# The shared expert's activation is split without its product with ones, and the last step's splits change places

## What is computed

```python
def _gate(x, gate_w, gate_bias):
    ...                      # 8 of 64 experts a token, their weights
    return (tidx, tw * SCALE)
w_dense = jnp.zeros((T, E), tw.dtype).at[jnp.arange(T)[:, None], tidx].add(tw)
def body(acc, ws):
    wg, wu, wdn, cw = ws
    hmid = jax.nn.silu(x @ wg) * (x @ wu)
    return (acc + cw[:, None] * (hmid @ wdn), None)
y, _ = jax.lax.scan(body, jnp.zeros_like(x), (We_gate, We_up, We_down, w_dense.T))
shared = jax.nn.silu(hidden_states @ Ws_gate) * (hidden_states @ Ws_up) @ Ws_down
return y + shared
```

## Time and profile before

| | us |
|---|---|
| median of three runs | 858.88 |
| lowest and highest | 857.32, 859.14 |
| the profiled execution | 856.9 |
| its span, first to last instruction | 855.1 |
| PE busy within it | 831.7 |
| of the page's chain that ended last, PE | 86% |

### The profile page before, as it was taken

How to read it: one execution, slowest core, us unless ns; L and a number is a source line. 1 busy time by engine, 2 the same in 40 slices (tenths; PEclk the granted TensorE clock), 3 DMA queues, 4 the chain that set the end, 5 groups by cost and what they waited for, 6 DMA issues and landing times.

```text
span 855.1 us, 20312 instructions
## 1 busy us (share of the span) xinstructions
PE 831.7 (97%) x6781; PEld 652.9 (76%) x6781; DVE 684.0 (80%) x1641; ACT 568.5 (66%) x967; POOL 641.2 (75%) x606
## 2 busy tenths in 40 slices
PE   7999999999999999999999999999999999999997
PEld 5577767777766678888888888878888888888885
DVE  6899989999897779769679787867987967876665
ACT  4488888888878765575576566557557557655554
POOL 2778888888853478877777886877787778778785
PEclk8699999999999999999999999999999999999999
DMA  5667787877652266547456555654654745656562
GB/s 146 173 150 175 176 178 168 196 163 176 139 129 51 68 137 173 127 116 171 126 140 146 133 136 139 155 122 111 158 143 111 183 118 141 142 119 147 137 141 55
DMA packets 108035, 120.03 MB, mean 140 GB/s; under 512 B 28560, under 2 KB 70352, under 8 KB 106496
## 3 DMA queue, kind: packets, MB, share of 16 engines
q1 hardware_dynamic: 104816, 117.64, 57.8%
q10 hardware_dynamic: 3120, 1.18, 0.7%
HBM read 103.55 MB, written 14.71 MB: 138 GB/s over the span
## 4 chain that ended last, share of the span: by engine, by line
PE 86%; DMA 4%; DVE 4%; issue 2%; SPq 2%; ACT 1%; POOL 0%; DVEq 0%; ACTq 0%; POOLq 0%
PE bank L2019 20%; PE bank L2020 20%; PE bank L2021 20%; PE bank L1348 7%; PE bank L1335 5%; PE bank L1306 3%; PE bank L1288 2%; PE bank L1356 2%; PE bank L1272 1%; DMA stack_k<-k_scratch 1%; PE bank L1369 1%; PE bank L1282 1%; DMA k_scratch<-parts_k 1%; SPq L376 1%; DMA cwb<-wts_scratch 1%
## 5 line engine op out<-in xcount | busy, mean ns | idle before, releaser
L1696 POOL TENSOR_TENSOR hid<-act,cwb 128x512 f32<-128x512 f32 x264 | 425.2, 1620 | 124.3 <-DVE act L1923 69.6
L1749 ACT ACTIVATE silu<-bank 128x512 f32<-128x512 f32 x256 | 152.9, 597 | 191.9 <-PE bank L2021 187.7
L1923 DVE TENSOR_TENSOR act<-silu,bank 128x512 f32<-128x512 f32 (+1 forms) x264 | 180.4, 684 | 117.0 <-ACT silu L1749 77.4
L2019 PE MATMUL bank<-xhi,weights_hi 128*128 128x512 f32 x520 | 206.6, 397 | 0.5 <-ACT silu L1749 0.5
L1931 DVE TENSOR_TENSOR hlo<-hid,hhi 128x512 fp32r<-128x512 f32 x256 | 200.8, 785 | 7.1 <-ACT hhi L1755 6.9
L2021 PE MATMUL bank<-xlo,weights_hi 128*128 128x512 f32 x520 | 204.1, 393 | 0.0
L2020 PE MATMUL bank<-xhi,weights_lo 128*128 128x512 f32 x520 | 204.0, 392 | 0.0
L1755 ACT ACTIVATE hhi<-hid 128x512 fp32r<-128x512 f32 (+1 forms) x264 | 164.8, 625 | 14.0 <-POOL hid L1696 12.0
L1005 DVE TENSOR_REDUCE mx<-bank 128x4 f32<-128x512 f32 x240 | 156.0, 683 | 16.7 <-PE bank L1306 15.0
L796 ACT ACTIVATE prob<-bank 128x1024 f32<-128x1024 f32 x128 | 131.2, 1025 | 45.4 <-PE bank L1335 43.4
L2019 PEld LDWEIGHTS bank<-xhi,weights_hi 128*128 128x128 f32 x520 | 97.6, 188 | 22.1 <-ACT silu L1749 1.1
(11 more groups left out here) (242 smaller groups left out, 1037.4 us busy)
## 6 DMA issues: line engine op xcount, KB each, us to landing
cwb<-wts_scratch SPq DMA_DIRECT2D x174, 384.0 KB, 5.4
stack_k<-k_scratch SPq DMA_DIRECT2D x30, 256.0 KB, 4.4
k_scratch<-parts_k SPq DMA_DIRECT2D x15, 384.0 KB, 3.6
stack_q<-q_scratch SPq DMA_DIRECT2D x30, 128.0 KB, 2.9
stack_k<-k_scratch SPq DMA_DIRECT2D x30, 128.0 KB, 5.2
q_scratch<-parts_q SPq DMA_DIRECT2D x15, 192.0 KB, 3.4
xin<-in_x_dram SPq DMA_DIRECT2D x16, 128.0 KB, 2.9
cin<-in_ctx_dram SPq DMA_DIRECT2D x16, 128.0 KB, 3.1
```

The lines of the kernel that those rows point to most:

```text
L1696: pool.tensor_tensor(h_buf[k][:], a_buf[k][:], cwb[slot][:, q % GP, :], ALU.mult).then_inc(h_ok, 1)
L1749: act.activation(s_buf[k % RS][:], g_bank[k % 2][:], ACT.Silu).then_inc(s_ok, 1)
L1923: nc.vector.tensor_tensor(a_buf[k % RS][at], s_buf[k % RS][at], u_bank[k % 3][at], ALU.mult).then_inc(a_ok, 1)
L2019: nc.tensor.matmul(bank, w[0], mh, start=first, stop=False)
```

## The change

Three things, in words:

- The shared expert's activation is no longer multiplied by ones on POOL. ACT and DVE split `act` itself (`a_buf`) instead of `hid` (`h_buf`). POOL makes 32 products a chunk instead of 33, `h_ok` counts 32 a chunk, and all counts that are compared with it are changed. ACT's splits now name the product count as a value of their own (`done`). DVE gets a wait in step q = 2, that the split of the shared expert has read `act` before its buffer is written anew.
- The rows of ones are gone: `wT`, `f_wT` and `wts_scratch` have 64 rows, the write of ones on POOL and its waits are gone, and the last group of `cwb` in a chunk has two pairs instead of three.
- In the very last step of the last chunk, ACT does hhi of the third last pair ahead of the silu instead of after it, and DVE does its hlo ahead of the last act instead of after it.

```diff
@@ the write of ones, in the attention, on POOL @@
-                if n == NC - 2:
-                    pool.wait_ge(st_mm, UNITS * b)
-                    pool.wait_ge(xb_ok, n + 1)
-                    pool.memset(f_wT[E:NEX, :], 1.0).then_inc(fc_ok, 1)
-                    pool.wait_ge(fc_ok, 3)
@@ SP @@
         def load_cwb(c, gr, slot):
-            wait(sp, h_ok, NP * c + GP * (gr - 1))
+            wait(sp, h_ok, (NP - 1) * c + (GP * (gr - 1) if gr else -2))
+            q0, q1 = GP * gr, min(GP * (gr + 1), NP - 1)
             for half in range(2):
-                sp.dma_start(cwb[slot][half * F:(half + 1) * F, :, :],
-                             wts_v[c][half][GP * gr:GP * (gr + 1)].unsqueeze(0).to_broadcast([F, GP, T])
+                sp.dma_start(cwb[slot][half * F:(half + 1) * F, 0:q1 - q0, :],
+                             wts_v[c][half][q0:q1].unsqueeze(0).to_broadcast([F, q1 - q0, T])
                              ).then_inc(cw_in[slot], 16)
@@ POOL @@
-                for q in range(NP):
+                for q in range(NP - 1):
                     hidden(NP * c + q, q, j, g)
@@ ACT @@
-        def hid_hi(n, k):
-            at = slice(F if k % NP == NP - 1 else 0, P)
-            wait(act, h_ok, n + 1)
+        def hid_hi(n, k, done):
             wait(act, dn_mm, n + 1 - RH)
-            act.activation(hhi[k % RH][at], h_buf[k % RS][at], ACT.Copy).then_inc(hh_ok, 1)
+            if k % NP == NP - 1:
+                wait(act, a_ok, n + 1)
+                act.activation(hhi[k % RH][F:P], a_buf[k % RS][F:P], ACT.Copy).then_inc(hh_ok, 1)
+                return
+            wait(act, h_ok, done)
+            act.activation(hhi[k % RH][:], h_buf[k % RS][:], ACT.Copy).then_inc(hh_ok, 1)
...
-                    silu(n, k)
+                    end = not more and q == NP - 1
+                    if not end:
+                        silu(n, k)
                     if not (first and q < 2):
-                        hid_hi(n - 2, k - 2)
+                        hid_hi(n - 2, k - 2, (NP - 1) * c + max(q - 1, 0))
+                    if end:
+                        silu(n, k)
@@ DVE @@
-            wait(dve, h_ok, n + 1 - RS)
+            wait(dve, h_ok, hidden)
+            if k % NP == RS - 1:
+                wait(dve, hl_ok, n + 1 - RS)
...
-                nc.vector.tensor_tensor(hhi[k % RH][0:F], h_buf[k % RS][F:P], hhi[k % RH][F:P].bitcast(F32),
+                nc.vector.tensor_tensor(hhi[k % RH][0:F], a_buf[k % RS][F:P], hhi[k % RH][F:P].bitcast(F32),
...
-                    act_up(n, k, (NP - 1) * c + q)
+                    end = not more and q == NP - 1
+                    if not end:
+                        act_up(n, k, (NP - 1) * c + q, (NP - 1) * c + q + 1 - RS + (q < RS - 1))
...
                         hid_lo(n - 2, k - 2)
+                    if end:
+                        act_up(n, k, (NP - 1) * c + q, (NP - 1) * c + q + 1 - RS + (q < RS - 1))
```

More of the change, by code:

```diff
@@ L136, in build @@
         gwT = keep("gwT", [P, E], F32)
-        wts_d = nc.dram_tensor("wts_scratch", (NB // 4, NEX, 4 * P), F32, kind="Internal").ap()
+        wts_d = nc.dram_tensor("wts_scratch", (NB // 4, E, 4 * P), F32, kind="Internal").ap()
         cw_base = keep.at
@@ L269, in attention @@
     f_wsel, f_wnorm = f_masked, f_rep
-    f_wT = m_late("f_wT", [NEX, T], F32)
+    f_wT = m_late("f_wT", [E, T], F32)
     warm = m("warm", [P, 1], F32)
@@ L845, in first_wT @@
             act.wait_ge(fwt_mm, 1)
-            act.wait_ge(fc_ok, 3)
-            act.activation(f_wT[0:E, :], misc[0][0:E, :], ACT.Copy).then_inc(fwt_ev, 1)
+            act.activation(f_wT[:], misc[0][0:E, :], ACT.Copy).then_inc(fwt_ev, 1)
         evac_t(0, 0)
@@ L1740, in evac_w @@
             wait(act, wt_st, 16 * (c - 1))
-            act.activation(wT[0:E, :], misc[0:E, :], ACT.Copy).then_inc(wt_ev, 1)
+            act.activation(wT[:], misc[0:E, :], ACT.Copy).then_inc(wt_ev, 1)
         def silu(n, k):
@@ L1793, in on_act @@
         for q in range(2):
-            hid_hi(NP * NCH - 2 + q, 2 * NP - 2 + q)
+            hid_hi(NP * NCH - 2 + q, 2 * NP - 2 + q, (NP - 1) * NCH)
         wait(act, dn_mm, NP * NCH)
@@ L1915, in route, with act_up @@
                 tt(wnorm[:], wsel[:], wsum_p.unsqueeze(2).to_broadcast([P, K, E]), ALU.mult).then_inc(w_ok, 1)
-        def act_up(n, k, ups):
+        def act_up(n, k, ups, hidden):
             at = slice(F if k % NP == NP - 1 else 0, P)
```

## The result

| | before | after |
|---|---|---|
| median, 22 runs each | 857.17 | 860.75 |
| lowest and highest | 855.6, 859.54 | 857.7, 864.46 |
| the profiled execution | 856.9 | 862.24 |
| its span | 855.1 | 860.3 |

After takes 1.0041 times as long as before, with a 95% interval of 1.0031 to 1.0050: it is slower by 3.6 us. Its runs also spread wider, over 6.8 us for 3.9. The forecast was 857.9, in a range up to 860.0, with 0.08 for a slower kernel. The last step did become shorter, as forecast. But at the loop's turn, where the engines jump back to the start of its body, PE loses more than the change gains.

What follows compares the result with a forecast made beforehand. PE, busy 97% of the span, was taken as the bound. Gains of 0.90 us (last step) and 0.05 (rows of ones), all else 0, sum to 0.95, from a median of 858.88 to 857.9 us; range 856.0 to 860.0.

Steps and rivals of the forecast that it cites:

- The last step: End of the last chunk: without the eighth product and with the exchange, PE's last down starts 0.90 us earlier (0.6 to 1.3).
- Seven products at the chunks' ends: Chunk ends before another chunk: removing POOL's 1.8 us shared-expert products is hidden by PE's own work, worth 0.
- The slower rival: Loop's turn: ACT's body, grown by 64 instructions, makes a second code-fetch stand in each of two turns; 860.3 us, chance 8%.
- The rival of a shorter turn: Loop's turn: with less for POOL to do, PE's loss of some 1.2 us goes; gain 2.2, 856.7 us, chance 8%.
- The exchange alone: Last step: reordering silu, act and splits is itself worth -0.1 us; the product's removal brings all of the gain.
- The rows of ones: First chunk: 64 rows for 66 shorten the weights' store, 0.05 us reaching PE; dropping POOL's write of ones is worth 0.
- the added waits: ACT's extra register instruction per loop step and DVE's wait in step q = 2 fall in slack: cost 0.
- The signs named ahead: Trace signs at the last step, chunk ends, loop's turn and on POOL; a new ACT stand without releaser would refute the prediction.
- The long split: Last step, DVE: hlo of the third last pair takes about 1.7 us, not 0.69.
- the late act: Last step, DVE: the last act starts about 0.9 us later than silu allows.
- POOL's relief: Whole kernel: POOL's busy time falls by some 14 us.
- the stall at the turn: Loop's turn: PE's stall stays near 0.5 us.

## Why the prediction was wrong

**Seven products at the chunks' ends, worth 0.** This is the step that failed, and in it one sentence: "The loads of the next weights start up to one product sooner [...]; both give POOL slack that PE doesn't see." The first half is what happened, the second asked only who waits for the load. At the loop's turn nobody waited for it: it stood in the way of something else, DVE's code, whose stand grew from 2.76 to 5.66 us. At the other chunks' ends, where no engine jumps, the products' removal was worth 0 as said. That it is the load, by way of DVE's jump, is shown by the load held back (stand 2.89, 857.18), the load made earlier in before (3.94, 859.15) and DVE without a jump (PE idle 0.16, 856.51). The change's other suspect at this place, longer code on ACT, leaves DVE's stand at 2.93 and PE's loss within some tenths of before's. Each kernel has one profile, so how much the stand varies from one execution to the next isn't known.

**The slower rival** named the right place and nearly the right time, 860.3 for 860.75. That was luck twice over. It started from 858.88, where the 22 runs of before give 857.17, so that it forecast a loss of 1.4 us for the 3.6 measured. And its reason was wrong: a second stand of ACT by code longer by over a quarter. ACT's body grows by 8 instructions in 368. ACT's stand in after is 3.39, shorter than before's 4.25, and the stand that counts is DVE's. What spoke against it, that ACT runs a chunk with no such stand, was right. But the earlier trace rows had shown ACT standing 3.40 us with nothing to wait for, and the question that this row raises, what the fetch competes with and who else fetches there, wasn't put. DVE's row of the same kind, idle before act at the turn in before, would have answered the second half:

```profile
572.95 0.69 DVE L1923 TENSOR_TENSOR act<-silu,bank 128x512 f32<-128x512 f32 x1 [2.48 <-ACT silu L1749]
```

The profile puts these 2.48 us down to silu on ACT, which came last by a little. DVE's own stand of 2.76 lay right behind it.

**The rival of a shorter turn** (gain 2.2) had the sign wrong. POOL isn't in that stall, as said against it.

**The last step.** The mechanism was right, and the term a little too large: a gain of 0.66 us for 0.90. DVE, then ACT and PE, which answer to the earlier trace rows:

```profile
850.18 2.38 DVE L1935 TENSOR_TENSOR hlo<-hid,hhi 128x512 fp32r<-128x512 f32 x2
852.59 0.69 DVE L1927 TENSOR_TENSOR act<-silu,bank 64x512 f32<-64x512 f32 x1
853.31 0.69 DVE L1935 TENSOR_TENSOR hlo<-hid,hhi 128x512 fp32r<-128x512 f32 x1
854.03 0.69 DVE L1932 TENSOR_TENSOR hhi<-act,hhi 64x512 fp32r<-64x512 f32 x1
...
853.37 0.63 ACT L1750 ACTIVATE hhi<-act 64x512 fp32r<-64x512 f32 x1 [0.64 <-DVE act L1927]
...
854.86 0.42 PE L2048 MATMUL bank<-hhi,weights_hi 128*128 128x512 f32 x1
```

```profile
L1935 DVE TENSOR_TENSOR hlo<-hid,hhi x2: 693/1236/1778, 850.8 to 853.3; 128x512 fp32r<-128x512 f32 x2
```

The split that was moved ahead takes 1778 ns, for 1.77 forecast, and holds the last act back, as it held its successors in the earlier trace rows. It again ends 0.55 us after POOL's product, which runs from 850.34 for 1.67. Up to that end, 2.08 us into the stretch, the sum was right to 0.01. What it had too small are the links behind: I let act start 0.07 before the split's end, and it starts 0.03 behind it (852.59); and from act's end to the last down I had 1.46 and it takes 1.58. There I let the second last pair's split start 0.08 before act's end, and it starts 0.03 behind (853.31). PE's second last down follows that split, and the last one follows PE without idle time at 854.86. Together 0.22 of the 0.24. The Trainium skill tells of an exclusive lock on the ports that VectorE and GpSimd share in "SBUF — State Buffer", section "SBUF: two separate sides". The trace agrees: 1778 and 1783 ns where a product is under way, 693 and 684 where none is.

**The exchange alone** was forecast at −0.1 us and is −0.36 (4.38 with it, 4.02 without); the product's removal alone is then +1.02. With the product kept, it costs 1.06. It is DVE's half that costs.

**The rows of ones, the added waits.** The profile after has the first down's stall at 1.98 us for 1.06, but in the others PE's longest stall there lies between 0.57 and 1.61 whatever the kernel: 0.05 us can't be seen in that. That ACT's added register instructions cost 0 is borne out away from the turn: but for the 0.4 near 622 us, which no other profile has, nothing moved in the rest of the phase.

**The signs named ahead.** The long split, the late act and POOL's relief came; the stall at the turn didn't stay near 0.5. ACT showed no new stand, and it was DVE on which one grew.

## What to carry to other kernels

A transfer that starts earlier isn't free because nobody waits for it: ask what else is to pass through memory in those microseconds, the code of an engine that jumps back over a long body included. In each trace, look up every engine's stand at each turn, also of those that the profile doesn't name as the releaser, and when its packets of kind instruction run. If a stand there is on the path, unroll the loop on that engine or hold the transfer back until the jump is over. Instructions put ahead of a step for which the last chain waits cost their own time and whatever lock they run into, so where removing work shortens that chain, try the removal without the exchange.

## What the runs showed of the hardware

- After a jump back, DVE (517 instructions in the body) stands 2.76 to 2.93 us where no load was issued just ahead of the jump, and 3.94 to 5.75 where one was. In the first case, five profiles, an instruction packet of 8 KB starts 0.96 to 0.98 us behind the jump. With the early load in before it is 2.07, and with that in after 3.16 to 3.49. From the last such packet's end to DVE's next instruction it is 1.24 to 1.62 us in all of them. So the stand contains a fetch of code, and what the loads lengthen is mainly the time until its packet runs. That a given packet is DVE's is inferred from its place; no row names the engine.
- ACT (368 to 432 instructions) stands 3.3 to 4.5 us at its jump, while the loads of the new chunk's first group are under way: its packet starts 2.32 us behind the jump before, and 1.39 in after, where the stand is 0.87 us shorter. POOL (222 or 216) stands 0.25 us and SP (178) 0.27, in every kernel that loops there, and PE, with the longest body (some 1330), 0.06. So length alone doesn't decide who stands, and no run here says what does.
- PE's idle time of 3.3 to 3.9 us at the turn was accompanied by the lower clock for 3.41 us in after and in both variants with the same turn. In after it fell 0.36 us behind the restart at 578.31, in the variant without the exchange 0.59 us ahead of the restart at 577.08. Idle times of 1.2 us and less there were not. In the first chunk idle times of up to 1.61 us were not either, and after has the one case of 1.98:

```profile
305.31 0.57 PE L2027 MATMUL bank<-hhi,weights_hi 128*128 128x512 f32 x1 [1.98 <-DVE hlo L1935]
...
305.00:309.00 4.00, 3.69 (x9) 2.93 (x10) 3.75 (x6) 3.29 (x7) 3.88 (x3) 0.58 0.26 60
```

- Matmuls start some 227 ns apart in the even chunks and 233 in the odd ones (medians), in all profiles. No run here says why.
